# DLRM tower on one core: halved last layers, weights in pieces, a third layer in strips, one bank for ScalarE alone, raw integer ids against row numbers

## The reference

```python
e = jnp.stack([tbl_0[ids[:, 0]], ..., tbl_26[ids[:, 26]]], axis=1)     # (2048, 27, 128) f32
z = einsum('bfd,bgd->bfg', e, e)[:, TRIL_I, TRIL_J]                    # (2048, 351)
h = concatenate([z, dense_ctx], axis=1)
h = maximum(h @ W_top1 + b_top1, 0)
h = maximum(h @ W_top2 + b_top2, 0)
y = h @ W_top3                                                         # (2048, 1)
```

## Time and profile before

| | us |
|---|---|
| median of 3 runs | 396.18 (391.86 to 401.06) |
| profiled execution | 398.12 |
| its span, first to last instruction | 396.2 |
| TensorE busy (matmuls) | 353.3 (89%) |
| GpSimd busy | 280.2 (71%) |
| VectorE busy | 264.3 (67%) |
| ScalarE busy | 212.2 (54%) |
| mean granted TensorE clock | 0.974 |

### The profile page before, as it was taken

The page is one execution under the profiler, slowest core; times in us unless marked ns, Lnnn a source line. Parts: engine busy times, 40 slices in busy tenths (PEclk is TensorE's granted clock), DMA queues, the critical chain, the costliest instruction groups (busy, mean ns, idle before and its releaser), DMA issues.

```text
span 396.2 us, 14625 instructions
## 1 busy us (share of the span) xinstructions
PE 353.3 (89%) x6180; PEld 321.6 (81%) x6180; DVE 264.3 (67%) x1044; ACT 212.2 (54%) x435; POOL 280.2 (71%) x286
## 2 busy tenths in 40 slices
PE   0876859999999969999999999999899999999677
PEld 0776849998789858998889888998799788997465
DVE  2999956992689454993779647992689457933310
ACT  3456273655647481563837483755447382746612
POOL 4887777777877777777777778777777777776030
PEclk9998968999999998999999999999999999999989
DMA  7984453224132522225232522234222422221000
GB/s 271 360 255 135 99 188 84 56 72 149 48 77 61 165 57 58 73 64 157 57 83 59 162 58 76 50 107 121 55 78 61 112 52 55 58 64 51 3 13 2
DMA packets 19602, 37.71 MB, mean 95 GB/s; under 512 B 6793, under 2 KB 8401, under 8 KB 19537
## 3 DMA queue, kind: packets, MB, share of 16 engines
q0 software_dynamic: 8896, 17.89, 17.2%
q1 hardware_dynamic: 8704, 16.00, 12.6%
q10 hardware_dynamic: 1936, 2.89, 2.2%
HBM read 35.88 MB, written 0.01 MB: 91 GB/s over the span
## 4 chain that ended last, share of the span: by engine, by line
PE 64%; POOL 16%; issue 7%; DMA 6%; SPq 3%; DVE 3%; ACT 2%; ACTq 0%
PE fill_ps L441 16%; PE fill_ps L442 16%; POOL rows L402 16%; PE pair_ps L458 10%; PE mlp_ps L471 7%; PE mlp_ps L497 6%; PE fill_ps L424 5%; DMA rows<-tbl_d,ids_sb 3%; SPq L313 3%; PE mlp_ps L504 2%; PE fill_ps L486 2%; DVE work L343 1%; DMA work<-work 1%; ACT et L551 1%; DMA ids_sb<-ids_d 1%
## 5 line engine op out<-in xcount | busy, mean ns | idle before, releaser
L402 POOL DMA_INDIRECT rows<-tbl_d,ids_sb x272 | 276.3, 1016 | 86.5 <-issue 80.2
L441 PE MATMUL fill_ps<-one_hot,table_hi 128*128 128x256 f32 x720 | 183.8, 294 | 14.1 <-DVE one_hot L654 14.1
L442 PE MATMUL fill_ps<-one_hot,table_lo 128*128 128x256 f32 x720 | 178.9, 288 | 0.0
L654 DVE TENSOR_SCALAR one_hot<-hot_ids 128x256 fp32r<-128x256 f32 x720 | 166.7, 303 | 13.1 <-PE fill_ps L442 12.3
L441 PEld LDWEIGHTS fill_ps<-one_hot,table_hi 128*128 128x128 f32 x720 | 141.8, 197 | 16.0 <-issue 14.0
L442 PEld LDWEIGHTS fill_ps<-one_hot,table_lo 128*128 128x128 f32 x720 | 141.9, 197 | 0.2
L343 DVE COPY work<-pair_ps 26x112 f32<-26x112 f32 (+1 forms) x256 | 66.0, 258 | 90.0 <-PE pair_ps L458 86.8
L343 ACT COPY work<-pair_ps 26x112 f32<-26x112 f32 (+1 forms) x256 | 61.2, 239 | 84.2 <-PE pair_ps L458 81.5
L551 ACT COPY et<-fill_ps 128x512 f32<-128x512 f32 (+1 forms) x80 | 79.4, 1118 | 0.5
L563 ACT COPY et<-fill_ps 128x512 f32<-128x512 f32 x40 | 46.7, 1225 | 41.4 <-PE fill_ps L442 34.4
L458 PEld LDWEIGHTS pair_ps<-et 128*26 128x26 f32 x4096 | 46.2, 104 | 25.4 <-issue 16.1
(11 more groups left out here) (22 smaller groups left out, 62.8 us busy)
## 6 DMA issues: line engine op xcount, KB each, us to landing
hot_ids<-ids_hot_d SPq DMA_DIRECT2D x34, 256.0 KB, 3.8
rows<-tbl_d,ids_sb POOLq DMA_INDIRECT x272, 2.5
work<-tbl_d SPq DMA_DIRECT2D x4, 640.0 KB, 4.3
work<-tbl_d SPq DMA_DIRECT2D x4, 512.0 KB, 7.1
hot_ids<-ids_hot_d ACTq DMA_DIRECT2D x6, 256.0 KB, 8.9
w_sb<-w_d ACTq DMA_DIRECT2D x1, 768.0 KB, 5.4
w_sb<-tbl_d SPq DMA_DIRECT2D x1, 640.0 KB, 4.1
w_sb<-tbl_d SPq DMA_DIRECT2D x1, 512.0 KB, 11.7
```

The lines of the kernel that those rows point to most:

```text
L402: nc.gpsimd.indirect_dma_start(out=rows[:, t, c, :], out_offset=None, in_=tables[f], in_offset=bass.IndirectOffsetOnAxis(ap=ids_sb[:, tile ...
L441: nc.tensor.matmul(to, table_hi[:, CHUNK_AT[k] + c, :], hot, start=(c == 0), stop=False)
L442: last = nc.tensor.matmul(to, table_lo[:, CHUNK_AT[k] + c, :], hot, start=False, stop=(c == CHUNKS_OF[k] - 1))
L654: last = nc.vector.tensor_scalar(one_hot[:, (first + c - c0) % ONE_HOT_RING, :], ids, float(c), None, ALU.is_equal)
```

## The change

- **Ids.** localise_ids and its semaphore are gone. make_one_hots compares the raw int32 ids with chunk_row[:, at + c], a per-partition f32 scalar that holds the table row of this partition and chunk (an iota of 18 columns at the start), in place of an immediate.
- **Weights.** w1 comes in three DMAs, issued by ScalarE at ("cold", 0, 1, 0) to ("cold", 0, 1, 2); w2 in two halves and vectors at ("hot", 1, 2) and ("hot", 1, 3). All six are awaited ahead of the first layer 1.
- **Third layer in strips.** layer3 multiplies each tile's 128 columns by itself, tile 0 into partition 0 and tile 1 into partition 32 of the same PSUM columns; output takes two copies and comes after VectorE's copies of bank 3, not at the layer3 step.
- **A bank for ScalarE alone.** In groups 0 to 6 all of bank 2 is copied by ScalarE (16 copies), none by VectorE. In group 7 all of bank 1 is copied by VectorE. wait_moved counts accordingly.
- **Last group.** Its layers run in two halves of 128 columns. The z DMAs of the first half (SyncE 8, GpSimd 7) are issued once bank 1 is moved, those of the second (SyncE, GpSimd and ScalarE, 5 each) once bank 3 is. TensorE: layer1_last(0), layer2_last(0), layer1_last(1), layer3_last(0), layer2_last(1), layer3_last(1). The ten dummy matmuls are gone. layer2(6, 1) moves from ahead of bank 2 to between banks 2 and 3, and layer3(6) behind bank 3.

```diff
@@ order
-            steps += [("layer2", b, 0), ("pairs", g, 1)] + cold[1][2:] + [("layer2", b, 1)]
-    return steps + [("pairs", GROUPS - 1, 2), ("layer3", GROUPS - 2), ("pairs", GROUPS - 1, 3)]
+            steps += [("layer2", b, 0), ("pairs", g, 1)] + cold[1][2:]
+            if g < LAST:
+                steps.append(("layer2", b, 1))
+    return steps + [("pairs", LAST, 2), ("layer2", LAST - 1, 1), ("pairs", LAST, 3), ("layer3", LAST - 1)]
@@ new
+def strips_of(engine, g, bank):
+    alone = {("dve", 1): range(STRIPS), ("act", 1): range(0)} if g == LAST else {
+        ("act", 2): range(STRIPS), ("dve", 2): range(0)}
+    shared = range(2) if engine == "dve" else range(2, STRIPS)
+    return tuple(alone.get((engine, bank), shared))
+def lows_by(engine, t):
+    movers = (("sp", "pool"), ("sp", "pool", "act"))[t]
+    return ALL_LOWS[movers.index(engine)::len(movers)]
@@ sync
-                    complete_zt(sp, step[1], ALL_LOWS, z_in)
+                    complete_zt(sp, step[1], 0, COLS, ALL_LOWS, z_in)
+                elif step == ("pairs", LAST, 1):
+                    complete_zt(sp, LAST, 0, P, lows_by("sp", 0), z_last_in[0])
+                elif step == ("pairs", LAST, PAIR_BANKS - 1):
+                    complete_zt(sp, LAST, P, COLS, lows_by("sp", 1), z_last_in[1])
@@ gpsimd
+                nc.gpsimd.iota(chunk_row_int[:, at:at + width], pattern=[[1, width]], base=0,
                                channel_multiplier=width).then_inc(consts, 1)
@@ tensor
+            def layer1_last(t):
+                pe.wait_ge(z_last_in[t], 16 * (Z_MOVES - len(lows_by("pool", t))))
+                pe.wait_ge(z_last_by_pool[t], 16 * len(lows_by("pool", t)))
+                for m in range(K2):
+                    for c in range(CHUNKS):
+                        last = nc.tensor.matmul(fill_ps[m][:, t * P:(t + 1) * P], w1_sb[:, c, m * P:(m + 1) * P],
+                                                zt[:, c, t * P:(t + 1) * P], start=(c == 0), stop=(c == CHUNKS - 1))
+                    last.then_inc(h1_full, 1)
             def layer3(g):
                 for c in range(M2):
                     pe.wait_ge(h2_done, g * M2 + c + 1)
-                    last = nc.tensor.matmul(y_ps, w3_sb[:, c:c + 1], h2[:, c, :],
+                    for t in range(GROUP_TILES):
+                        last = nc.tensor.matmul(y_ps[t], w3_sb[:, c:c + 1], h2[:, c, t * P:(t + 1) * P],
+                                                start=(c == 0), stop=(c == M2 - 1))
...
-            for _ in range(WARM):
-                nc.tensor.matmul(mlp_ps[1][:, 0:COLS], w2_sb[:, 0, 0:P], h1[:, 0, :], start=True, stop=True)
-            layer1_last()
+            pe.wait_ge(fill_moved, len(FILL))
+            layer1_last(0)
             pe.wait_ge(y_done, LAST)
-            for m in range(M2):
-                layer2(LAST, m)
-            layer3(LAST)
+            layer2_last(0)
+            layer1_last(1)
+            layer3_last(0)
+            layer2_last(1)
+            layer3_last(1)
@@ scalar
+            def load_weights(step):
+                if step[0] == "cold" and step[1:3] == (0, 1) and step[3] < CHUNKS:
+                    c = step[3]
+                    act.wait_ge(lo_made, MOST_HOT)
+                    act.dma_start(w1_sb[:, c, :], w1[c * P:(c + 1) * P, :]).then_inc(w_in, 16)
+                elif step in (("hot", 1, 2), ("hot", 1, 3)):
+                    c = K2 // 2 * (step[2] - 2)
+                    act.dma_start(w2_sb[:, c:c + K2 // 2, :], w2[c * P:(c + K2 // 2) * P, :].rearrange(
+                        "(c p) n -> p c n", p=P)).then_inc(w_in, 16)
...
+            complete_zt(act, LAST, P, COLS, lows_by("act", 1), z_last_in[1])
@@ vector
-                ids = hot_ids[:, slot, (k - k0) * COLS:(k - k0 + 1) * COLS].bitcast(F32)
-                dve.wait_ge(hot_ids_local, localised_through(HOT_FILL[step]))
+                ids = hot_ids[:, slot, (k - k0) * COLS:(k - k0 + 1) * COLS]
+                at = sum(WIDTHS[:WIDTHS.index(CHUNKS_OF[k])])
+                dve.wait_ge(hot_ids_in[slot], 16 * (HOT_FILL[step] // IDS_RING + 1))
...
                         last = nc.vector.tensor_scalar(one_hot[:, (first + c - c0) % ONE_HOT_RING, :], ids,
-                                                       float(c), None, ALU.is_equal)
+                                                       chunk_row[:, at + c:at + c + 1], None, ALU.is_equal)
...
+                    if bank == PAIR_BANKS - 1 and g > 0:
+                        output(g - 1)
```

More of the change, by code:

```diff
@@ L107, with moved_through @@
 NEXT_HOT = {a: b for a, b in zip(list(HOT_FILL), list(HOT_FILL)[1:])}
+def strips_of(engine, g, bank):
[3 more added lines that the diff above has]
+    return tuple(alone.get((engine, bank), shared))
+def moved_through(engine, number):
+    return sum(1 for _, g, bank in list(BANK)[:max(number, 0)] if strips_of(engine, g, bank))
 def halves(k):
@@ L263, in build @@
         mlp_ps = [ctx.enter_context(nc.psum_tensor(f"mlp_ps{i}", [P, 512], F32)) for i in range(2)]
-        y_ps = mlp_ps[0][0:1, COLS:2 * COLS]
+        y_ps = [mlp_ps[0][STRIP * t:STRIP * t + 1, COLS:COLS + P] for t in range(GROUP_TILES)]
+        y_last_ps = [pair_ps[t][0:1, 0:P] for t in range(GROUP_TILES)]
         first_ids_in = sem("first_ids_in")
@@ L285, in build @@
         z_in = sem("z_in")
-        z_last_in = [sem(f"z_last_in{c}") for c in range(CHUNKS)]
-        dense_in = sem("dense_in")
+        z_last_in = [sem(f"z_last_in{t}") for t in range(GROUP_TILES)]
+        z_last_by_pool = [sem(f"z_last_by_pool{t}") for t in range(GROUP_TILES)]
         w_in = sem("w_in")
@@ L295, in build, with wait_moved, complete_zt @@
         stored = sem("stored")
-        N_W = 3
-        LAST = GROUPS - 1
+        N_W = CHUNKS + 3
         block = ctx.enter_context(nc.Block())
-        def complete_zt(engine, g, lows, landed):
-            engine.wait_ge(pair_moved_v, (g + 1) * PAIR_BANKS)
-            engine.wait_ge(pair_moved_a, (g + 1) * PAIR_BANKS)
+        def wait_moved(engine, number):
+            wait_count(engine, pair_moved_v, moved_through("dve", number))
+            wait_count(engine, pair_moved_a, moved_through("act", number))
+        def complete_zt(engine, g, c0, c1, lows, landed):
+            wait_moved(engine, BANK["pairs", g, c1 // (COLS // PAIR_BANKS) - 1] + 1)
             for low in lows:
@@ L335, in move_pairs @@
         def move_pairs(engine, g, bank, strips, moved, copy):
+            if not strips:
+                return
             engine.wait_ge(pair_full, BANK["pairs", g, bank] + 1)
@@ L499, in layer2, with layer2_last @@
                 last.then_inc(h2_full, 1)
+            def layer2_last(t):
+                for m in range(M2):
+                    for c in range(K2):
+                        if m == 0:
+                            pe.wait_ge(h1_done, (LAST + t) * K2 + c + 1)
+                        last = nc.tensor.matmul(mlp_ps[m][:, t * P:(t + 1) * P], w2_sb[:, c, m * P:(m + 1) * P],
+                                                h1[:, c, t * P:(t + 1) * P], start=(c == 0), stop=(c == K2 - 1))
+                    last.then_inc(h2_full, 1)
             def layer3(g):
@@ L614, in _ @@
                     relu2(step[1], step[2])
+            complete_zt(act, LAST, P, COLS, lows_by("act", 1), z_last_in[1])
             for m in range(K2):
-                relu1(LAST, m)
+                relu1_last(0, m)
             for m in range(M2):
-                relu2(LAST, m)
+                relu2_last(0, m)
+            for m in range(K2):
+                relu1_last(1, m)
+            for m in range(M2):
+                relu2_last(1, m)
         @block.vector
@@ L687, in _ @@
                     if bank == 0:
-                        wait_count(dve, z_in, g * (16 * MOVES))
-                    move_pairs(dve, g, bank, (0, 1), pair_moved_v, nc.vector.tensor_copy)
-                elif step[0] == "layer3":
-                    output(step[1])
-            output(LAST)
+                        wait_count(dve, z_in, g * (16 * Z_MOVES))
+                    move_pairs(dve, g, bank, strips_of("dve", g, bank), pair_moved_v, nc.vector.tensor_copy)
+                    if bank == PAIR_BANKS - 1 and g > 0:
+                        output(g - 1)
+            dve.wait_ge(stored, 16 * LAST)
+            for t in range(GROUP_TILES):
+                output_last(t)
 def kernel(**inputs):
```

119 lines of the change are left out of this document (46 added, 73 removed).

## The result

The changed kernel takes 456.9 us (median of 4 runs, 453.56 to 461.05) against 398.62 for the kernel before beside it: a ratio of 1.157, 95% interval 1.133 to 1.180. The forecast was 389.5 us. The profiled execution has a span of 459.2 us against 396.2, so there are 63.0 us to find. (On some chips single executions of a kernel, of the one before too, come out longer at a lower granted clock; every ratio here leaves them out, so that a median and a ratio beside it need not fit.)

What follows compares the result with a forecast made beforehand. Back-to-back GpSimd gathers were taken as the bound, TensorE a close second. Span 396.2 - 5.3 (tail) - 3 (gathers) = 387.9, 389.8 for the execution; 6.7 off the 396.18 median gave 389.5 us, range 383 to 402.

Steps and rivals of the forecast that it cites:

- The bound: GpSimd's 272 gathers run back to back, a chain of 358.9 us that no data holds up; TensorE a close second.
- the part on the third layer in strips: Layer 3 in each group: TensorE gains 0 to 3 us, worth nothing; VectorE no longer waits in mid-stream for y.
- The gathers' term: GpSimd's gathers beside VectorE's one-hots: -3 us in sum from changed delays.
- the steps of 0.08: Small delays of gathers beside one-hots, 9.5 us before; with longer compares 9 to 19, so 0 to +9.
- The two long gathers: Gathers of 2.48 and 2.47 us beside id subtractions; they lose their cause: 2 x 1.53 = -3.1 us.
- Rival (a): Longer compares hold gathers back in one-hot stretches, 1.53 us per stall, two a group: 410 us; chance 0.15.
- the 2.02 us of the earlier trace: A gather beside a two-input table_lo subtraction; said not to fit the skill page's inference that descriptor writing is free of it.
- The compares' price: VectorE's 720 one-hot compares take 60 ns more, pace 0.26 us for 0.22: 29 us more.
- the ring of 20 covers the unevenness: no cost: VectorE's 30 us of work per group fits in 44 us of gathers, with the one-hot ring covering unevenness: no cost.
- rival (c): Compares leave the fast mode and the gathers alone; 5.5 us off until TensorE binds: 387, or 385 from the median; chance 0.15.
- The tail: Halved layers of the last group end at 389.0 against 394.3: -5.3 us, bounds -7 and -2.
- Weights in pieces and the bank for ScalarE alone: Weights: one wait of 0 to 3 us in group 1, nothing at the end. Bank 2: 2 us more for ScalarE, nothing waits.

Runs made afterwards that it cites:

- e15: The kernel before with only VectorE's copies of y moved behind its copies of bank 3, directly ahead of the compares: 457.25 us, ratio 1.151.
- e10: The kernel before with the ids' part of the change alone: 406.69 us, ratio 1.029.
- e9: The changed kernel with the ids' part undone (id subtractions and float immediates again): 439.34 us, ratio 1.118.
- e11: The changed kernel with int32 ids compared with an immediate in place of the per-partition scalar (one-hots wrong): 427.41 us in one execution.
- e13: The changed kernel with one wait more, VectorE waiting for its copies of y to finish before the compares: 393.2 us, ratio 0.991.
- e16: The changed kernel, ids undone, waiting behind y's copies, last group's ScalarE evictions of layer 1's first half ahead of its z loads: 402.57 us, ratio 0.999.
- e18: As e13, but all loads of z on SyncE and GpSimd, none on ScalarE, on a chip of 604 us: 625.69 us, ratio 0.992.
- e17: The same kernel as e13, repeated on another chip, of 604 us: 637.25 us against 604.14 for the kernel before.

## Why the prediction was wrong

**The bound** was right: gathers back to back were the chain that ends last, and their sum became the time, 67.3 of gathers and -3.7 of tail against 63.0 in all.

**The step that failed** is in the part on the third layer in strips: "VectorE no longer waits in mid-stream for y" was costed at nothing. The copies of y cost VectorE nothing; but they were moved directly ahead of its longest unbroken stretch, and e15 shows that this alone brings the six held gathers (a ratio of 1.151, with the two of group 0). I had asked what waits for y and what y waits for, and not what now begins right behind it. Before, the copies of pairs stood there, and the compares began 0.03 us after their end (kernel before, VectorE):

```profile
117.42 2.16 DVE L343 COPY work<-pair_ps 26x112 f32<-26x112 f32 x8
119.61 2.23 DVE L654 TENSOR_SCALAR one_hot<-hot_ids 128x256 fp32r<-128x256 f32 x10
```

**The gathers' term**, -3 us, measured +67.3. Its parts: the steps of 0.08, forecast at 0 to +9, came out at about -7 (98 of them became 8). The two long gathers did go. The six new ones were in no bound: the range allowed 1.53 us for a held gather, the longest excess that the trace of before held, and the real ones are seven to ten times that.

**Rival (a)** had the right mechanism on the right chain and a wrong cause, price and chance. It blamed the length of a compare; e10 has the long compares and no held gather, e9 the short ones and six. The price is the length of the stretch, 39 to 56 compares at 0.20 or 0.26 us, not that of an instruction. Its thresholds don't follow from its own numbers either: with 1.53 us each against the 6.7 us taken off the median, about 5 held gathers, not 9, make the change slower, and about 10, not 14, slower by 2%. The rule of the Trainium skill ("SBUF — State Buffer", "Who interferes with whom") points the same way, the loser being blocked for the whole instruction. The rows disagree with it in the length: blocked for 56 instructions in a row, of 334 ns each, and released when VectorE had a gap. That the port is what is held is that page's reading; the runs show only the times. Nor does the 2.02 us of the earlier trace rows settle anything about writing descriptors, as the prediction had it: a gather also reads its row numbers from ids_sb.

**The compares' price** of +60 ns was right (334 against 276 in e11), and so was its pace with no gather between them: 14.77 / 56 = 0.264 us. But with gathers between them it is 17.52 / 56 = 0.313, against the 0.22 of the earlier trace rows, and the sum of all 720 rises from 166.7 us to 223.6 in e10: 57 us on VectorE rather than 29. That is the term behind e10: VectorE, at 0.313, no longer stays ahead of TensorE ("the ring of 20 covers the unevenness: no cost"), and TensorE waits 25.1 us for it. In e13 the bank for ScalarE alone gives VectorE its 15 us back, and these waits are 18.9, of which 11.0 lie at the start as before. That these two parts belong together once no gather is held is likely by this, but no run has one without the other and everything else alike.

**What TensorE's slack is worth.** In e13 the last gather ends at 347.9 us, 16.6 earlier than in the trace of the kernel before (from another chip), and the ratio is only 0.991: the gathers' gain went into TensorE, whose waits hold none for a gather any more. That is what rival (c) said of its own gain, and (c)'s 385 still took too much of it.

**The tail** was forecast at -5.3 with bounds of -7 and -2, and measured -3.7. The halves of layers took nearly their forecast times at full clock: 24 passes in 2.94 against 2.6, 16 in 2.05 against 1.8. The other two had a granted clock of 0.70 and 0.75 on average, a part of each at the 1.2 GHz level, and took 2.86 instead of 2.05 and 3.72 instead of 2.94, which is 1.6 us together; the forecast held 1.7. Changed kernel, windows (length, TensorE busy, ..., granted clock, DMA share, GB/s):

```profile
447.60:450.50 2.90, 2.85 (x17) 2.88 (x18) 0.00 (x0) 1.05 (x4) 0.00 (x0) 0.70 0.04 8
450.30:454.00 3.70, 3.70 (x26) 3.58 (x26) 0.00 (x0) 1.47 (x4) 0.00 (x0) 0.75 0.00 0
```

The missed piece is in ScalarE's queue. Changed kernel, ScalarE and TensorE:

```profile
440.37 1.99 ACT L349 COPY work<-pair_ps 26x112 f32<-26x112 f32 x8 [0.74 <-PE pair_ps L467]
442.56 3.73 ACTq L317 DMA_DIRECT2D work<-work  x4
446.32 0.77 ACTq L313 DMA_DIRECT2D work<-dense_d  x1
447.14 1.14 ACT L599 ACTIVATE work<-fill_ps,vectors 128x128 f32<-128x128 f32 x4 [4.78 <-issue]
```

```profile
440.65 2.94 PE L490 MATMUL fill_ps<-work,w_sb 128*128 128x128 f32 x24
447.65 2.86 PE L507 MATMUL mlp_ps<-work,w_sb 128*128 128x128 f32 x16 [4.06 <-ACT work L599]
```

Layer 1's first half is done at 443.6, but its evictions stand behind five issues of 4.5 us, and TensorE waits 4.06. I had put five loads on "each of three queues" and counted only when they land. Yet e16 and e18 show that this isn't 4 us to be had: with the issues later or elsewhere the second half waits 3.7 and 2.6 us for its z.

**Weights in pieces and the bank for ScalarE alone** cost nothing visible: the waits of after have none for weights in layer 1, and none of the pairs for ScalarE's copies of bank 2.

## What to carry to other kernels

Here GpSimd's gathers could be held for a whole stretch of VectorE's compares. In such a kernel a tiny instruction moved directly ahead of a long unbroken stretch is to be priced at that stretch, each time round, and not at its own length. Where an engine that must stay ahead (gathers here) runs beside dense work, look in the trace for its single longest instructions, not their mean, and try a wait that costs a tenth of a microsecond ahead of the dense stretch; it helped where gathers followed each other closely, not where GpSimd asked late. When a part that an engine issues is moved, what stands behind it on that engine is a term of the sum.

## What the hardware showed that was not expected

- A gather of 0.94 us took up to 15.65 us beside unbroken compares, and ended 0.12 or 0.82 us after VectorE's last one; whether the compares began 0.07 us before or 0.04 us after the end of a copy of 0.28 us decided it, 18 of 18 held against 0 of 18, as long as gathers followed each other closely. Where GpSimd asked late (1.7 us into the stretch) it could be held in either case.
- A per-partition scalar costs a 256-wide compare 59 ns over an immediate (335 against 276), int32 input nothing; and once a gather is in, it takes its turns, and the compares' pace goes from 0.264 to 0.313 us.
- Two chips of this kind ran the same program in 604 us instead of 394 to 405; in e17 there 162 us of TensorE's waits are "issue" ahead of the pair matmuls. The edit worth 0.991 on the one kind brought no gain on the other: e17's six runs took 609.54 to 643.65 us against 600.6 to 614.86 of before.
